# A cross-attention and expert kernel: fewer warm-up products and an earlier routing in the row stage, GpSimd's share of the weight splitting moved into the first expert tiles

## The reference

```python
kv = ctx @ W_k.T + b_k
sim = ((layernorm(x) @ kv) @ kv.T) * 512 ** -0.5
sim = (sim - mean) * rsqrt(var + 1e-6) * gamma + beta
x = x + softmax(sim)
n = layernorm(x)
s, i = top_k(n @ Wg.T, 2); w = softmax(s)
for e in range(8):                      # H = 352
    h = silu(n @ W1[e].T) * (n @ W2[e].T)
    y = y + w[e] * (h @ W3[e].T)
x = x + y
```

## Time and profile before

| | us |
|---|---|
| median of 3 runs | 388.43 (388.06 to 389.5) |
| the profiled execution | 388.07 |
| its span, first to last instruction | 386.3 |
| PE busy | 356.9 (92%) |
| DVE busy | 267.9 (69%) |
| ACT busy | 268.2 (69%) |
| POOL busy | 171.6 (44%) |
| mean granted clock of TensorE | 0.967 of full |

### The profile page before, as it was taken

How to read it: one execution, slowest core, us unless ns; L and a number is a source line. 1 busy time by engine, 2 the same in 40 slices (tenths; PEclk the granted TensorE clock), 3 DMA queues, 4 the chain that set the end, 5 groups by cost and what they waited for, 6 DMA issues and landing times.

```text
span 386.3 us, 8154 instructions
## 1 busy us (share of the span) xinstructions
PE 356.9 (92%) x2277; PEld 233.2 (60%) x2277; DVE 267.9 (69%) x661; ACT 268.2 (69%) x467; POOL 171.6 (44%) x202
## 2 busy tenths in 40 slices
PE   5999999998896778889999999999999999999981
PEld 4656676776653545556666666666666666666640
DVE  1268688857976999995757576666767575757660
ACT  1289999979696978976666657575666666666650
POOL 2124856659934135545253434344343435253331
PEclk9999999998776999999999999999999999999997
DMA  6999999999503123255544445353536354544423
GB/s 194 416 383 409 347 382 403 369 317 372 204 3 84 28 57 55 56 86 88 104 66 99 76 91 84 81 90 79 99 66 109 61 106 66 100 73 95 80 30 54
DMA packets 21945, 57.60 MB, mean 149 GB/s; under 512 B 4816, under 2 KB 4944, under 8 KB 20368
## 3 DMA queue, kind: packets, MB, share of 16 engines
q0 software_dynamic: 8736, 20.53, 29.6%
q1 hardware_dynamic: 12016, 30.27, 21.2%
q10 hardware_dynamic: 1152, 6.29, 4.6%
HBM read 38.17 MB, written 18.91 MB: 148 GB/s over the span
## 4 chain that ended last, share of the span: by engine, by line
PE 55%; DVE 6%; issue 4%; DMA 1%; ACT 1%; DVEq 1%; POOLq 0%; ACTq 0%
PE bank L1251 32%; PE bank L1285 17%; PE bank L1242 4%; PE bank L1271 3%; DVE stage L983 2%; DVE Wp L833 2%; DMA out<-kvj_s,sidx 1%; DVE x_s L1015 1%; DVE kvg_s L989 1%; ACT stage L677 1%; DVE n_s L1007 0%; POOLq L74 0%; DVE wsel L999 0%; DVEq L996 0%; DVE wmul L1003 0%
## 5 line engine op out<-in xcount | busy, mean ns | idle before, releaser
L983 DVE SCALAR_TENSOR_TENSOR stage<-W,w3sc,stage 128x512 f16<-128x512 f16 x117 | 84.2, 747 | 6.5 <-ACT stage L677 5.9
L1285 PE MATMUL bank<-stage,n_s 128*128 128x512 f16 (+1 forms) x351 | 82.2, 379 | 3.5 <-DVE n_s L1007 2.0
L1251 PE MATMUL bank<-Wp,kvg_s 128*128 x480 | 80.2, 318 | 4.8 <-DVE kvg_s L989 4.8
L677 ACT ACTIVATE stage<-W,w3sc 128x512 f16 x117 | 80.1, 717 | 0.0
L1251 PE MATMUL bank<-Wp,kv_s 128*128 x456 | 74.3, 313 | 2.0 <-DVE kv_s L989 2.0
L511 POOL DMA_INDIRECT out<-oT_s,sidx x20 | 34.2, 1712 | 75.9 <-ACT oT_s L704 68.7
L1251 PEld LDWEIGHTS bank<-Wp,kvg_s 128*128 128x128 f16 x480 | 47.5, 99 | 32.2 <-issue 6.7
L511 POOL DMA_INDIRECT out<-kvj_s,sidx x19 | 32.4, 1707 | 66.1 <-ACT kvj_s L704 63.5
L1251 PEld LDWEIGHTS bank<-Wp,kv_s 128*128 128x128 f16 x456 | 44.5, 98 | 26.6 <-issue 3.0
L1007 DVE TENSOR_TENSOR n_s<-bank,n_s 128x384 f16<-128x384 f32 x39 | 21.7, 557 | 55.3 <-ACT n_s L690 55.3
L1285 PEld LDWEIGHTS bank<-stage,n_s 128*128 128x128 f16 (+1 forms) x351 | 34.2, 98 | 36.7 <-issue 3.9
(11 more groups left out here) (189 smaller groups left out, 553.8 us busy)
## 6 DMA issues: line engine op xcount, KB each, us to landing
Wp<-in_w SPq DMA_DIRECT2D x8, 1408.0 KB, 11.2
W<-in_w ACTq DMA_DIRECT2D x8, 768.0 KB, 7.6
stage<-in_xT SPq DMA_DIRECT2D x4, 1024.0 KB, 8.2
W<-in_x SPq DMA_DIRECT2D x12, 256.0 KB, 8.6
out<-W SPq DMA_DIRECT2D x12, 256.0 KB, 9.5
n_table<-n_s SPq DMA_DIRECT2D x8, 256.0 KB, 7.6
n_table<-x_s SPq DMA_DIRECT2D x8, 256.0 KB, 6.3
stage<-in_x SPq DMA_DIRECT2D x4, 256.0 KB, 9.2
```

What stands on the lines that cost most here:

```text
L677: eng.activation(w3p[t % 2][:, c * D:(c + 1) * D], W3[:, bass.ds(e * W3N + c * D, D)], ACT.Copy, scale=w3sc[:, bass.ds(e, 1)]).then_inc(s_ ...
L983: eng.scalar_tensor_tensor(w3p[r][:, W3N + c * D:W3N + (c + 1) * D], W3[:, bass.ds(e * W3N + c * D, D)], w3sc[:, bass.ds(e, 1)], w3p[r][:, ...
L1251: mm = eng.matmul(bank[2 * which + r][:, 0:H], n_, w_, start=(c == 0 and k == 0), stop=(c == DC - 1 and k == 2))
L1285: mm = eng.matmul(ybank(t - 1)[:, :], h_, w_, start=(c == 0 and k == 0), stop=(c == HC - 1 and k == 2))
```

## The change

- **Warm products.** Start 30 to 55; per slot 8 to 2 of 128 columns, but four and eight times `WARM_SLOT` between the first steps, as many as before; from slot 11 on 12 to 4 of 384 columns (8 from slot 14); the last warm of the drain halved; 20 to 36 before the first gather's rows, and 10 more behind their transposes (`WARM_ROWS`).
- **Row stage.** ctxT is loaded first. `squares` takes an expert's up weights in one instruction of 2816 columns, in every second slot. The `turned` copy of odd row groups under 12 moves to DVE. `gram`, `gram_copy` and `centre_keys` come a slot earlier.
- **Routing.** Five groups instead of four batches, of 4, 4, 4, 2 and 2 row groups; `places` and `columns` of group 0 in slots 12 and 13, of group 1 in 15 and 16; `number(0)` and `number(1)` on ACT in slots 14 and 16; `table(0)` in slot 15.
- **Low parts.** `first_low` on POOL goes; DVE makes `w12_low(0, 0)`, ACT `w12_high(0, 0)` later. For the experts 3 to 7 POOL makes the last 704 of the 2816 columns (`part_low`, two instructions) between its gather and its scatter, DVE's second half is 704 instead of 1408 columns, and PE waits for both. `low_rows` comes ahead of `w12_low`.
- **First tile.** `turn_rows(0)` ahead of the product over the w3 squares; `w12_high(1, 0)` ahead of `mT_evac(0)`.

```diff
+HELP_FROM = 3
+HELP = 2 * H
-WARM_GATHER = 20
+WARM_GATHER = 36
+WARM_ROWS = 10
-WARM_SLOT = 8
-WARM_LATE = 12
-WARM_START = 30
+WARM_SLOT = 2
+WARM_LATE = 4
+WARM_LAST = 8
+WARM_START = 55
+GROUPS = ((0, 4), (4, 4), (8, 4), (12, 2), (14, 2))
...
+        def by_vector(g):
+            return g % 2 == 1 and g < G - TPB
...
-            eng.dma_start(bk_s[:, :], bk).then_inc(s_bk, 16)
-            for dst, src in ((wk_s[:, :], wkT), (ctx_s[:, 0:N], ctxT[:, 0:N])):
+            for dst, src in ((ctx_s[:, 0:N], ctxT[:, 0:N]), (wk_s[:, :], wkT)):
                 eng.dma_start(dst, src).then_inc(s_key, 16)
+            eng.dma_start(bk_s[:, :], bk).then_inc(s_bk, 16)
...
-            first_low()
...
+            def part_low(k):
+                cols = slice(W12N - HELP, W12N)
+                high = Wp[:, 2 * k * W12N:(2 * k + 1) * W12N]
+                low = Wp[:, (2 * k + 1) * W12N:(2 * k + 2) * W12N]
+                eng.wait_ge(s_hi, 2 * k + 2)
+                eng.tensor_scalar(wst[k][:, cols], wst[k][:, cols], wscale[:, k:k + 1], None, ALU.mult).then_inc(s_lopt, 1)
+                eng.wait_ge(s_lopt, k - HELP_FROM + 1)
+                eng.tensor_tensor(low[:, cols], wst[k][:, cols], high[:, cols], ALU.subtract).then_inc(s_lop, 1)
             for t in range(NT):
                 gather(t + 3)
+                if HELP_FROM <= t + EARLY < E:
+                    eng.wait_ge(s_lo, 2 * (t + EARLY))
+                    part_low(t + EARLY)
                 eng.wait_ge(s_y, t + 1)
...
-                if row(s - 4):
+                if row(s - 4) and not by_vector(s - 4):
                     turned(s - 4)
...
-                if 0 <= s + 3 < 2 * E:
-                    squares((s + 3) // 2, (s + 3) % 2)
+                if (s + 2) % 2 == 0 and 0 <= (s + 2) // 2 < E:
+                    squares((s + 2) // 2)
...
+                if s == 14:
+                    number(0)
                 if s == 16:
-                    w12_high(0, 0)
+                    number(1)
...
             turned(G - 3)
-            number(0)
             turned(G - 2)
             router_exp(0)
             turned(G - 1)
-            number(1)
+            w12_high(0, 0)
+            w3_square(2)
+            number(2)
             w12_high(0, 1)
-            number(2)
-            w3_square(2)
+            number(3)
             w3_square(3)
             router_exp(1)
...
+            w12_high(1, 0)
             mT_evac(0)
-            w12_high(1, 0)
...
+                if h == 1:
+                    wait(eng, s_lop, k - HELP_FROM)
+                cols = slice(h * WH, (h + 1) * WH - (HELP if h == 1 and k >= HELP_FROM else 0))
...
+            def turned(g):
+                eng.wait_ge(s_nTp, g + 1)
+                eng.wait_ge(s_scp, g + 1)
+                eng.tensor_copy(nT_s[:, g % 2, :], bank[6][:, :]).then_inc(s_nTv, 1)
...
+                if s == 12:
+                    places(0)
+                if s == 13:
+                    columns(0)
                 if s == 15:
-                    places(0)
+                    places(1)
                 if s == 16:
                     weight_scale()
-                    columns(0)
+                    columns(1)
...
-            places(1)
             chosen(G - 4)
-            columns(1)
             chosen(G - 3)
+            classes(3)
+            class_sums(3)
             places(2)
             chosen(G - 2)
             columns(2)
             chosen(G - 1)
-            classes(3)
-            class_sums(3)
+            classes(4)
+            class_sums(4)
+            places(3)
+            columns(3)
-            places(B - 1)
-            columns(B - 1)
+            places(NG - 1)
+            columns(NG - 1)
...
-                    w12_low(t + EARLY, 0)
                     if t > 0:
                         low_rows(t + 1)
+                    w12_low(t + EARLY, 0)
...
-            eng.wait_ge(s_lo, 1)
+            w12_low(0, 0)
             w12_low(0, 1)
...
-                    warm(wide, WARM_LATE)
-                if s == 12:
+                    warm(wide, WARM_LATE if s < 14 else WARM_LAST)
+                if s == 11:
                     rank(0)
+                if s == 14:
+                    rank(1)
...
-            table(0)
+            rank(3)
             router(G - 1)
             table(1)
-            rank(3)
+            rank(4)
             counts()
             table(2)
-            warm(wide, WARM_DRAIN)
             table(3)
+            warm(wide, WARM_DRAIN // 2)
+            table(4)
...
                         eng.wait_ge(s_lo, 2 * t + 2)
+                        wait(eng, s_lop, t - HELP_FROM + 1)
...
+            eng.wait_ge(s_idx, 2)
+            turn_rows(0)
+            warm(oh[:, :, :, :].rearrange("p g k e -> p (g k e)"), WARM_ROWS, 7)
             eng.wait_ge(s_w3q, E)
```

More of the change, by code:

```diff
@@ L260, in build @@
         s_sct = sem("s_sct")
+        s_lopt, s_lop = sem("s_lopt"), sem("s_lop")
         NCONST = 21
@@ L284, in batch_at, with turned_ready @@
             return b if (s - i) % TPB == 0 and real(b) else None
+        def by_vector(g):
+            return g % 2 == 1 and g < G - TPB
+        def turned_ready(eng, g):
+            if by_vector(g):
+                eng.wait_ge(s_nTv, sum(by_vector(i) for i in range(g + 1)))
+            elif g >= 0:
+                eng.wait_ge(s_nT, sum(not by_vector(i) for i in range(g + 1)))
         def score_bank(g):
@@ L293, in ring_free @@
             eng.wait_ge(s_op, B)
-            wait(eng, s_tab, q - 1)
+            wait(eng, s_tab, min(q - 1, 2))
         def ybank(t):
@@ L609, in number @@
                 eng.wait_ge(s_ohp, q + 1)
-                for i in range(TPB):
+                g0, m = GROUPS[q]
+                a = g0 // TPB % 2
+                for i in range(m):
                     cols = slice(i * TOPK, (i + 1) * TOPK)
-                    eng.activation(oh_r[:, q % 2, :, cols], oh_r[:, q % 2, :, cols], ACT.Copy,
-                                   scale=tok1[:, q * TPB + i:q * TPB + i + 1]).then_inc(s_ohn, 1)
+                    eng.activation(oh_r[:, a, :, cols], oh_r[:, a, :, cols], ACT.Copy,
+                                   scale=tok1[:, g0 + i:g0 + i + 1]).then_inc(s_ohn, 1)
             def router_exp(part):
@@ L619, in router_exp, with squares @@
                 eng.activation(edl[:, g0:g1], dlt[:, g0:g1], ACT.Exp).then_inc(s_ed, 1)
-            def squares(k, h):
+            def squares(k):
                 eng.wait_ge(s_w[k], 16)
-                wait(eng, s_wq, 2 * k + h)
-                eng.activation(wjunk, wst[k][:, h * WH:(h + 1) * WH], ACT.Square,
-                               accum_out=wsq[:, k, h:h + 1]).then_inc(s_wq, 1)
+                wait(eng, s_wq, k)
+                eng.activation(wjunk, wst[k], ACT.Square, accum_out=wsq[:, k:k + 1]).then_inc(s_wq, 1)
             def w12_high(k, h):
@@ L867, in slot @@
                     scale_in(s)
+                if row(s - 5) and by_vector(s - 5):
+                    turned(s - 5)
                 b = batch_at(s, 3, 1)
@@ L1068, in counts @@
             def counts():
[L1070 to L1073 removed]
+                eng.wait_ge(s_wmax, 1)
+                eng.wait_ge(s_cs, NG)
+                for q in range(NG):
+                    mm = eng.matmul(bank[1][:, 0:E], ones16[:, :], csum[:, q, :], start=(q == 0), stop=(q == NG - 1))
                 mm.then_inc(s_cntp, 1)
             def table(q):
[L1078 removed]
+                g0, m = GROUPS[q]
                 i0, a = g0 % TPB * TOPK, g0 // TPB % 2
                 eng.wait_ge(s_ohc, q + 1)
[L1081 to L1082 removed]
+                if q < NG - 1:
+                    eng.wait_ge(s_ohn, g0 + m)
                 else:
@@ L1137, in turn_n @@
                 eng.wait_ge(s_n, g + 1)
-                wait(eng, s_nT, g)
+                turned_ready(eng, g - 1)
                 for c in range(DC):
@@ L1158, in slot @@
             def slot(s):
-                b = batch_at(s, 1, 1)
-                if b:
-                    gram(b)
-                b = batch_at(s, 0, 1)
-                if b is not None:
-                    turn_keys(b)
+                first = batch_at(s, 0, 1)
+                if first is not None:
+                    turn_keys(first)
                 b = batch_at(s, 2, 2)
@@ L1190, in slot @@
                     sims(s + 3)
-                b = batch_at(s, 0, 1)
-                if b is not None:
-                    outs(b)
+                if first is not None:
+                    outs(first)
                 if row(s - 3):
                     turn_n(s - 3)
+                if first:
+                    gram(first)
                 if s == 13:
                     weight_norms()
+                if s == 15:
+                    table(0)
             eng.wait_ge(s_const, 1)
@@ L1292, in _ @@
             eng.wait_ge(s_et, 1)
-            eng.wait_ge(s_idx, 2)
-            turn_rows(0)
             for t in range(NT + 1):
```

73 lines of the change are left out of this document (29 added, 44 removed).

## The result

The changed kernel took 411.19 us (410.76 to 420.73, median of 4 runs), the kernel before 388.25 beside it: ratio 1.0587, 95% interval 1.0543 to 1.0631. It is 23 us slower; forecast were 384.4 us, with a range to 390. The profiled execution spans 409.8 us, at a mean granted clock of 0.931. Where the granted clock fell low in some executions of a kernel, the ratio leaves those out, so it can differ from the median.

The account below looks back on a forecast made before the run. PE was taken to bound the last 32 tiles, PE, ACT and DMA the row stage, DVE the first tiles. -2.0 -4.0 -2.0 -0.5 +4.5 = -4.0 gave 384.1, as median 384.4 us, range 377 to 390.

Parts of the forecast that it names:

- Start, -2.0: Start of the kernel: 25 more warm products hidden in PE's wait and ctxT first save 2.0 us (0 to 3.2).
- Row stage, -4.0: Row stage: fewer warm products save 3.0 and, late, 1.8 us; number on ACT costs 0.8; sum -4.0.
- Drain, -2.0: Drain, where routing is closed: ACT's shorter list and moved steps save 2.0 us together (0 to -5).
- ACT sets the end of the drain: Drain: ACT's list, not the routing, ends it; that list was put at -2.1 us.
- First up, -0.5: First up product: 3.70 us at half speed; WARM_ROWS can restore it, but DVE sets the pace: -0.5 (0 to -1.9).
- Help, +4.5: First tiles: POOL's share of DVE's low parts costs 4.5 us, bounds -3.7 and +7.2.
- The price of contention on DVE: First tiles: blocking by POOL puts 1.7 to 2.2 us a tile on DVE, against 0.73 saved; +4.7 to +7.2.
- the loop's price: First tiles: POOL's loop allows 7.2 to 8.2 us per tile against 7.46; five tiles -1 to +4.
- Low rows, 0: First tiles: low rows ahead of L833 change nothing while DVE is full.
- (A): Rival, first tiles: the help helps, POOL does the waiting; -2 instead of +4.5, so 378; chance 0.27.
- (C): Rival, first tiles: DVE's back-to-back run starves POOL, up waits 3.8 us more per tile; 396; chance 0.09.
- (B): Rival: start and row stage give little, for DMA or the clock; -1.0 instead of -6.0, 389.4; chance 0.17.

Follow-up runs that it names:

- e15: Kernel before plus ctxT loaded first, 55 warm products at the start, 2 small ones a slot, low_rows ahead of w12_low: 384.95 us, ratio 0.9922.
- e5: Changed kernel without the help on GpSimd and with gram, gram_copy and centre_keys in the slots of before: 386.44 us, ratio 0.9972 to the kernel before.
- e3: Changed kernel with gram, gram_copy and centre_keys back in the slots of before, help kept: 396.96 us, ratio 1.0166 to the kernel before.
- e1: Changed kernel with no low part on GpSimd, VectorE making all of them again: 399.11 us, ratio 1.0267 to the kernel before.
- e7: Kernel before with only gram_copy one slot earlier in DVE's queue: 396.47 us, ratio 1.0202.
- e8: Kernel before with only centre_keys one slot earlier in DVE's queue: 391.68 us, ratio 1.0085.
- e6: e5 with the row stage's warm products of before (8 a slot, 12 wide from slot 11): 390.32 us, ratio 1.0043 to the kernel before.
- e11: e5 with 12 wide warm products in slots 11 to 15: ratio 1.0024 to the kernel before.
- e12: e5 with each weight square in two instructions again, one per slot: ratio 1.0029 to the kernel before.
- e13: e5 with all copies of turned rows on ACT again: ratio 1.0049 to the kernel before.
- e18: e17 plus joined weight squares and the odd row copies on VectorE: 382.09 us, ratio 0.9872 to the kernel before.
- e16: e15 plus the changed kernel's drain without its groups: 382.93 us, ratio 0.9849 to the kernel before.
- e17: e16 with router_exp(1) ahead of the last w3_squares on ACT: 380.94 us, ratio 0.9827 to the kernel before.
- e9: e3 with part_low one iteration earlier in GpSimd's queue, ahead of the scatter: 391.37 us, ratio 1.0073 to the kernel before.
- e14: Kernel before with only low_rows moved ahead of w12_low on DVE: 386.59 us, ratio 0.9954.
- e2: Changed kernel with the row stage's warm products of before: 412.84 us, ratio 1.0521 to the kernel before.
- e10: e5 with router_exp(1) ahead of w3_square(3) and mT_evac(0) ahead of w12_high(1, 0) on ACT: ratio 0.9953 to the kernel before.

## Why the prediction was wrong

**Start, -2.0: right, as far as can be told.** `keys` is 1.08 us long, `outs` starts 3.1 us sooner (2.3 in e15, 2.7 in e5), and at batch 3 e15 and e5 are 2.0 and 1.8 us ahead. No run has the start alone; that all of it is the start's follows only if the slots between gave nothing.

**Row stage, -4.0: the step that failed.** The sum prices products, squares, copies, `number` and `places`, but has no term for `gram_copy` and `centre_keys` a slot earlier in DVE's queue, though the change names them. A step moved forward in an in-order queue takes its wait with it. Undone, it is worth 14 to 16 us (e3), 11 to 13 where the help is gone too (e5 against e1); put alone into the kernel before, 7.9 and 3.3 (e7, e8). The other terms came to little as well: with the order restored, batch 0 to batch 3 takes 45.8 us (57.24 - 11.43) against 44.9, though PE and ACT have room. The products are worth 2.1 us there (e6, with them back, takes 47.9), but nothing is left of it. In that stretch of e5 only DMA is full:

```profile
41.20:59.07 17.87, 15.90 (x95) 11.07 (x94) 14.76 (x57) 15.75 (x31) 11.04 (x21) 1.00 1.03 377
```

The prediction had read DMA at 1.01 as one of three full resources and yet counted 3.0 of 4.6 us. But that DMA holds the slots isn't shown: no run made the loads lighter, and between 24 and 57.24 us of e5 no wait of an engine ends with a load; the longest pass from DVE and ACT to POOL (8.6 us in 6 waits, 4.1 in 3). What holds them stays open. The late slots take 38.0 us (57.24 to 95.21) in e5 and 36.2 in e15. e11, e12 and e13 (37.7 to 37.8) rule out clock, squares and copies as the cause, and e18, which has both of the last but not the five groups and the moved `places`, `columns` and `number`, takes 36.7 (57.43 to 94.08); so these cost 1.1 to 1.3 us together, where the sum had 0.8 for `number`.

**Drain, -2.0: right in size where it stands alone, lost in the changed kernel.** With the batches' groups as before, the drain edits give 3.1 to 3.6 us (e16, e17 against e15's 25.5), and ACT's last square does come sooner. In the changed kernel the drain took 25.9 us, 0.4 more than before. "ACT sets the end of the drain" holds no longer there: the first gather does. Timelines of ACT, POOL and PE in the changed kernel, then of POOL in e16:

```profile
120.38 0.23 ACT L646 ACTIVATE edl<-dlt 128x4 f32<-128x4 f32 x1
...
130.79 0.60 ACT L698 ACTIVATE kvg_s<-bank 128x512 f16<-128x512 f32 x1 [0.86 <-PE bank L1284]
```

```profile
125.37 2.29 POOL L506 DMA_INDIRECT ng_s<-n_table,gidx  x1 [3.09 <-issue]
```

```profile
130.12 0.63 PE L1284 MATMUL bank<-ident,ng_s 128*128 128x128 f32 x4 [0.87 <-DMA ng_s<-n_table,gidx]
```

```profile
110.10 1.24 POOL L489 DMA_INDIRECT ng_s<-n_table,gidx  x1 [2.95 <-DVE sidx L951]
```

The gather starts 2.5 us behind L995, which makes its indices (122.86). By the code it also waits for the store of the router weights, which follows ACT's second exp, and it starts 5.0 us behind that exp, as in e1, e3, e5 and e16 (4.7 to 5.1). The exp stands behind the squares and comes 14.0 us after the last norm, in e16 11.5. And the gather lasts 2.29 us instead of 1.24, while DVE's `w12_low(0, 0)` is under way. The start costs 2.5 us against e16 (19.0 and 16.5 us after the last norm), the length 1.1: that is the whole difference of 3.4 us. The prediction named both, the store behind `router_exp(1)` and the low part that can hold up the gather, and priced neither; its 1.8 us for 16 more warm products are those of full clock, while the 36 take 6.6 us here. Why the exp comes so late stays open: e5, with the same drain code, has it 12.0 us after the last norm and takes 23.9.

**First up, -0.5: about right.** In e17 it takes 1.96 us instead of 3.70, but from it to the `up` of tile 2 are 13.9 us against 14.5 in e15, where it still takes 3.70: 0.6 us of the 1.7 arrive.

**Help, +4.5: direction right, size wrong.** It cost 12 (8 to 11 with the DVE order restored, e3 against e5). The loop was put at 14.3 to 16.4 us per two tiles and measured 18.1: scatter 9.65 us after `up` instead of 8.9, and L523 and L525 together 5.1 us (169.95 to 175.05) instead of 2.5 to 3.4. The estimate took 1.9 for the first of them, where half of L451's 4.28 is 2.14, and priced no blocking into the loop: where DVE hardly interferes, the two take 2.07 and 1.52 us, here 2.61 and 2.41. The price of contention on DVE, 1.7 to 2.2 us a tile, was right: e9 isolates it, 8.13 us a tile against 7.13 with 0.73 less work, 1.7, which are the 1.23 of L1039 and the 0.51 of L1023. Choosing between the loop's price and the contention's was the error, for in the loop both stand. The Trainium skill, "SBUF — State Buffer", "Who interferes with whom", says of a VectorE instruction in a mode that uses both port pairs, which `tensor_scalar` can enter, that it or the GpSimd instruction, whichever issues first, keeps the shared pair to its end and the other blocks; L1039, a `tensor_scalar`, at 1.51 us beside L525's 1.52 agrees, though no trace shows its mode.

**Low rows, 0: wrong.** e14 measures 1.8 us (0.9 to 2.6) in their favour. "DVE is full" was read from 50.12 of 52.50 us; the order takes PE's wait of 1.00 us in a tile away, and a tile falls from 7.46 to 7.13 us.

**Rivals.** (A) fell with e1. (C), the other side with 0.09, named POOL's starving and 15 us; its wait of PE over 3 us came in every second tile, but more by the place in POOL's queue than by blocking, which lengthens L523 and L525 by 1.4 us for two tiles, where (C) had 3.8 in each. (B)'s outcome, that start and row stage give little, is what e5 shows: 0.2 us at the last norm instead of 6. Its reason isn't the clock: that did fall from 77 to 98.8 us (0.80 in the changed kernel, 0.84 in e5), but e11 has it full and wins 0.2 us, and e2 brought the products back and won nothing that can be told.

## What to carry to other kernels

When a step is moved forward in an in-order queue, ask first when its input is ready, by the producer's row, and who stands behind it: a copy of 0.29 us cost 8 (e7). When help for a full engine is put on another queue, add the wait ahead of its place and both engines' blocking, and do not choose between them. Take a change apart before you drop it: four of its parts and an earlier exp make a kernel 1.7% faster (e17). And before two stages are compared, look at how far the same code spreads: this drain took 23.9 to 28.9 us.

## What the runs showed of the hardware

Beside a GpSimd instruction on 704 columns (L525, 1.52 us) a VectorE one on two columns lasted 1.50 to 1.51 us instead of 0.28, five times in e9. GpSimd's other one, L523, took 3.33 to 3.41 us beside VectorE's low parts in four of five cases of e9, 2.07 at 178.46 in the changed kernel. The first gather's instruction on GpSimd took 2.23 to 2.54 us where a VectorE low part of 1408 columns was well under way (e5: 2.43, begun 0.37 us behind it), 1.24 and 1.25 before it (e10, e16, e17); but the second of e17 took 0.96, begun 0.03 us behind one. On 8 columns GpSimd's power (L513) took 3.03 us in e5, begun 0.17 us behind a VectorE low part, and 1.66 in e10, where a low part began 0.51 us behind it and took its usual 1.69.
